# Shared expert: last inner chunk with gate and up in one stationary tile, row transposes and logits issued later

## The chip, the cores and the metric

The kernel runs on one core of a Trainium2 chip. The metric is the device time of one execution in microseconds (us), the median of several runs; lower is better. The core has five engines with queues of their own: TensorE (PE; its weight loads are shown as PEld), VectorE (DVE), ScalarE (ACT), GpSimd (POOL) and SyncE (SP), which here only issues DMAs. They run in order and meet through semaphores.

## The reference, cut to what matters

x has 4 x 1024 rows of 256; the context has 77 keys per batch.

```python
x = x + tanh(g_xattn[0]) * xattn(layernorm(x), ctx, ctx, mask, w_q, b_q, w_k, b_k, w_v, b_v, w_o, b_o)  # 16 heads of 16
x = x + tanh(g_ffn[0]) * ffn(layernorm(x), gate_w, eg, eu, ed, sg, su, sd)

def ffn(x, ...):                                   # H = 256, I = 688, 4 experts, top 2
    scores = softmax(xf @ gate_w.T)                # the logits
    topk_w, topk_idx = top_k(scores, 2)            # normalised, spread into comb[n, e]
    y = sum_e comb[:, e] * ((silu(xf @ eg[e].T) * (xf @ eu[e].T)) @ ed[e].T)
    y = y + (silu(xf @ sg.T) * (xf @ su.T)) @ sd.T # the shared expert
```

## The kernel before, in words

There are three parts, one after the other: `attend_and_share` (attention, the second layernorm, the router's logits and the shared expert), `route_and_prepare` (top-2 routing and the experts' weights) and `feed_forward` (the routed experts, 67 tiles). The change touches the first alone.

The rows are cut into NU = 16 units of 256 rows (two tiles of 128). A software pipeline of 20 steps runs over them, and each engine has a `step(i)` of its own whose order is written out by hand. In step i, TensorE does for unit i the scores (four groups, j = 0 to 3), for unit i-1 the transposes of the probabilities (`prob_T`, five groups through the one bank `p_t`) and the product with the values (`prob_v`), for unit i-2 the output projection, the transposes of the normalised rows (`xn_T`, L893) and the logits (`logits`, L904), for unit i-3 the shared expert's gate and up products (`gate_up`, L913, six chunks c of the inner dimension), for unit i-4 the down product (`down`, L933), and for unit i+1 the transposes and the product for q. Steps 3 to 15 have all but the ends of this. Several of these go through the one PSUM bank `p_m` in turn: x_T, q_T (read by q_hi on ScalarE, L463, and q_lo on VectorE, L656), xn_T (read by `xn_copies` on ScalarE, L496), logits (read by `lg_copy`, L504), prob_v and the output projection. `prob_v(n)` waits until `lg_copy` has read the bank.

Matrix products of f32r data are made of three passes (high x high, high x low, low x high parts). The inner dimension of 688 is five chunks of 128 and one of FT = 48 rows. `gate_up(n, c)` does 2 (gate, up) x 2 (halves of 256) x 3 passes = 12 matmuls into one bank of `p_f`, gate in columns 0 to 255 and up in 256 to 511. In the last chunk the stationary tile holds the 48 weight columns twice (at 0 and at LO_AT = 64), so that the hidden rows appear twice; rows 64 to 111 of the last chunk of `hT[0]` then carry the low part (`last_lo`, L701, on VectorE), and `down` needs two matmuls for it in place of three.

After a chunk ScalarE takes the tanh (`gate`, L509), VectorE multiplies twice (`inner`, L690), ScalarE makes the high part (`h_hi`, L514) and GpSimd the low part (`h_lo`, L357). `half_max(n, j)` (L669, VectorE) makes the row maxima of a score group, `exps` (L471, ScalarE) the exponentials, `t_copy(n, g)` (L486, ScalarE) moves a group of transposed probabilities out of `p_t`, after which `prob_T(n, g + 1)` may start. `normalise` (L337) and `xn_lo` (L350) are GpSimd's. `gate_up(n, c)` waits until `inner(n, c - 2)` is done, its bank being free then; `down` waits for `h_lo` and `last_lo`.

The order of step(i) on TensorE around the change is: scores 2, gate_up 2, xn_T, prob_T 3, gate_up 3, logits, prob_T 4, scores 3, gate_up 4, gate_up 5, prob_v; then scores 0 of the next step, down, output projection. On ScalarE: t_copy 2, normed_2, h_hi 1, q_hi, gate 2, xn_copies, four exponentials of group 2, t_copy 3, gate 3, h_hi 2, lg_copy, the other four, t_copy 4, gate 4, h_hi 3, four exponentials of group 3, gate 5, h_hi 4, the last four, h_hi 5, normed. On VectorE: q_lo, half_max 2, inner 2, stats_1, inner 3, recip 2, half_max 3, inner 4, inner 5, no_sight, recip 3, last_lo.

Of the kernel before, what the change touches and what calls it, by code (L numbers as in the profile page):

```python
# [47 lines left out]

XR = 6
NE = N * TOPK // P  # L50
EG = 8
# [61 lines left out]
def attend_and_share(nc, allocator, v):  # L113
# [6 lines left out]
    with st:  # L120
# [110 lines left out]
        def w_group(w):  # L231
# [4 lines left out]
            return "d", 0, 2 * (w - 8), 2  # L236

        W_AT = {0: 6, 1: 5}

# [71 lines left out]
        def _(pool):  # L311
# [73 lines left out]
            for s in range(2):  # L385
                pool.memset(wgu[s][:, :, :, FF:FF + P // 2 - FT].bitcast(fp32), 0.0).then_inc(s_wpad, 1)
                pool.memset(wgu[s][:, :, :, FC * P - P // 2 + FT:FC * P].bitcast(fp32), 0.0).then_inc(s_wpad, 1)
            pool.memset(tail[:, :, :], 0.0).then_inc(s_wpad, 1)
            residual_bias(0)

# [7 lines left out]
            def step(i):  # L398
                if i == 1:
                    down_tail()  # L400
                if has(i + 1):
                    residual_bias(i + 1)
                if has(i - 2):
                    rstd2(i - 2)
                if has(i):
                    normalise(i, 0)
                if has(i - 3):
                    h_lo(i - 3, 0)
                if has(i):
                    normalise(i, 1)  # L410
                if has(i - 3):
                    h_lo(i - 3, 1)
                if has(i - 2):
                    xn_lo(i - 2)
                if has(i - 3):
                    h_lo(i - 3, 2)
                if has(i):
                    normalise(i, 2)
                if has(i - 3):
                    h_lo(i - 3, 3)  # L420
                if has(i + 2):
                    rstd1(i + 2)
                if has(i - 3):
                    h_lo(i - 3, 4)
                if i % UB in (1, 2) and i // UB + 1 < B:

                    b = i // UB + 1
                    wait(pool, s_S, 4 * UB * (b - 1))
                    for m in range(KC):
                        key_block(b, i % UB - 1, m, s_kbnext)  # L430
                if has(i):
                    normalise(i, 3)
# [5 lines left out]
        def _(act):  # L438
# [70 lines left out]
            def gate(n, c):  # L509
                act.wait_ge(s_F, FC * n + c + 1)  # L510
                wait(act, s_hid, FC * n + c - 1)
                act.activation(th[:, c % 2, :], f_bank(f_use(n, c))[:, 0:UT * P], ACT.Tanh, scale=0.5).then_inc(s_th, 1)

            def h_hi(n, c):  # L514
                act.wait_ge(s_hid, FC * n + c + 1)
                wait(act, s_D, n)
                act.activation(hT[0][:, c, :], hid[:, c, :], ACT.Copy).then_inc(s_hhi, 1)  # L517

            def w_hi(w):
# [6 lines left out]
                else:  # L526
                    j = "gu".index(kind)
                    full = min(FF - c0 * P, cn * P)
                    last = act.activation(wgu[0][:, k, j, c0 * P:c0 * P + full], bank[:, 0:full], ACT.Copy)
                    if c0:  # L530
                        at = FC * P - P // 2
                        last = act.activation(wgu[0][:, k, j, at:at + FT], bank[:, at - c0 * P:at - c0 * P + FT],
                                              ACT.Copy)
                last.then_inc(s_whi, 1)
# [20 lines left out]
            def step(i):  # L555
# [31 lines left out]
                for w in weights_in(i)[2:4]:  # L587
                    w_hi(w)
                if has(i - 2):
                    xn_copies(i - 2)  # L590
                if has(i):
# [6 lines left out]
                if has(i - 2):  # L598
                    lg_copy(i - 2)
                if has(i):  # L600
# [3 lines left out]
                if has(i - 3):  # L604
                    gate(i - 3, 4)
                    h_hi(i - 3, 3)
                if has(i):
                    exps(i, 3, 0, HH // 2)
# [16 lines left out]
        def _(dve):  # L625
# [64 lines left out]
            def inner(n, c):  # L690
                bank = f_bank(f_use(n, c))
                dve.wait_ge(s_th, FC * n + c + 1)
                nc.vector.scalar_tensor_tensor(out=ah[:, c % 2, :], in0=th[:, c % 2, :], scalar=1.0,
                                               in1=bank[:, 0:UT * P], op0=ALU.add, op1=ALU.mult).then_inc(s_ah, 1)
                dve.wait_ge(s_ah, FC * n + c + 1)
                if c < FC - 1:
                    wait(dve, s_hlo, (FC - 1) * (n - 1) + c + 1)
                nc.vector.tensor_tensor(hid[:, c, :], bank[:, UT * P:2 * UT * P], ah[:, c % 2, :],  # L698
                                        ALU.mult).then_inc(s_hid, 1)

            def last_lo(n):  # L701
                dve.wait_ge(s_hhi, FC * (n + 1))
                nc.vector.tensor_tensor(hT[0][LO_AT:P, FC - 1, :], hid[LO_AT:P, FC - 1, :], hT[0][LO_AT:P, FC - 1, :],
                                        ALU.subtract).then_inc(s_hlast, 1)

# [7 lines left out]
            def w_lo(w):  # L713
# [6 lines left out]
                else:  # L720
                    j = "gu".index(kind)
                    full = min(FF - c0 * P, cn * P)
                    last = nc.vector.tensor_tensor(wgu[1][:, k, j, c0 * P:c0 * P + full], bank[:, 0:full],
                                                   wgu[0][:, k, j, c0 * P:c0 * P + full], ALU.subtract)
                    if c0:
                        at = FC * P - P // 2
                        last = nc.vector.tensor_tensor(wgu[1][:, k, j, at:at + FT],
                                                       bank[:, at - c0 * P:at - c0 * P + FT],
                                                       wgu[0][:, k, j, at:at + FT], ALU.subtract)
                last.then_inc(s_wlo, 1)  # L730
# [89 lines left out]
        def _(pe):  # L820
# [92 lines left out]
            def gate_up(n, c):  # L913
                if c == 0:
                    pe.wait_ge(s_xnlo, n + 1)
                    pe.wait_ge(s_wlo, 11)
                    pe.wait_ge(s_wpad, 5)
                    wait(pe, s_hid, FC * n)
# [5 lines left out]
                bank = f_bank(f_use(n, c))  # L924
                for j in range(2):
                    for k in range(KC):
# [21 lines left out]
            def w_T(w):  # L948
# [15 lines left out]
                else:  # L964
                    for c in range(c0, c0 + cn):
# [3 lines left out]
                        else:  # L969
                            for at in (0, P // 2):  # L970
                                last = nc.tensor.transpose(bank[:, (c - c0) * P + at:(c - c0) * P + at + FT],
                                                           raw[kind][0:FT, c * H + k * P:c * H + (k + 1) * P],
                                                           ident[0:FT, 0:FT])
                last.then_inc(s_wtr, 1)
# [30 lines left out]
            def step(i):  # L1005
# [28 lines left out]
                for w in weights_in(i)[2:4]:  # L1034
                    w_T(w)
                if has(i - 2):
                    xn_T(i - 2)
                if has(i - 1):
# [3 lines left out]
                if has(i - 2):  # L1042
                    logits(i - 2)
                if has(i - 1):
# [3 lines left out]
                if has(i - 3):  # L1048
                    gate_up(i - 3, 4)
                    gate_up(i - 3, 5)  # L1050
                for w in weights_in(i)[4:]:
# [610 lines left out]
```

## Time and profile before

| | us |
|---|---|
| median of 3 runs | 1085.26 (1084.17 to 1085.97) |
| profiled execution | 1084.47 |
| its span | 1082.6 |

| engine | busy us | share of the span | instructions |
|---|---|---|---|
| PE | 971.2 | 90% | 6399 |
| PEld | 870.2 | 80% | 6400 |
| DVE | 561.7 | 52% | 1255 |
| ACT | 498.8 | 46% | 1806 |
| POOL | 471.4 | 44% | 641 |

The page gives the shares of the whole span. `attend_and_share` takes about the first 540 us, `feed_forward` runs from about 619 us to the end, and in both TensorE is busy over nine tenths of the time. The share of busy time is a mean over stages, so it doesn't say which wait ends last in a step; the timeline of one step does. In rows of the timeline the number in square brackets is the time that the engine stood idle before the instruction, and what ended it. Durations overlap: the next matmul may start before the one before it has ended.

### The profile page before, as it was taken

To read this page: it belongs to the slowest core of one execution; us is meant where nothing else is said; L and a number is where in the kernel's file an instruction comes from. 1 tells how busy PE (TensorE), PEld (TensorE's weight loads), DVE (VectorE), ACT (ScalarE), POOL (GpSimd) and SP (SyncE) were. 2 spreads that over 40 slices of the span, in tenths; PEclk is the share of its full clock that TensorE was granted. 3 is DMA by queue.
4 is the path that set the end of the run, shared out by engine and by line. 5 is a ranking of instruction groups with operands and counts; after the bars stand their busy time and mean duration, and the time that the engine had idled before them with its cause. 6 is when DMAs were issued, how large, how long until landed. Compare 5 with 4: busy or idle time off the path is not lost. (4 is left out here: it accounts for less than half of the span.)

```text
span 1082.6 us, 21517 instructions
## 1 busy us (share of the span) xinstructions
PE 971.2 (90%) x6399; PEld 870.2 (80%) x6400; DVE 561.7 (52%) x1255; ACT 498.8 (46%) x1806; POOL 471.4 (44%) x641
## 2 busy tenths in 40 slices
PE   5678999999999999999747599999999999999995
PEld 3457888888888888888636489999999999999995
DVE  4555555556565565643389544444444444444442
ACT  3777676677776767663122222222222222222221
POOL 4345445545554444333107434444444444444442
PEclk9789999999999999999956699999999999999999
DMA  5100102100111110000053112222222222222221
GB/s 175 34 18 14 34 3 57 33 19 26 36 33 33 33 33 21 11 30 21 21 181 105 51 25 39 39 39 39 39 40 40 40 39 39 39 40 37 44 39 20
DMA packets 47646, 44.92 MB, mean 41 GB/s; under 512 B 14618, under 2 KB 44159, under 8 KB 47583
## 3 DMA queue, kind: packets, MB, share of 16 engines
q0 software_dynamic: 12864, 17.57, 10.0%
q1 hardware_dynamic: 33655, 26.37, 8.1%
q8 instruction: 31, 0.51, 0.2%
q10 hardware_dynamic: 1064, 0.21, 0.1%
q14 instruction: 32, 0.26, 0.1%
HBM read 26.39 MB, written 17.43 MB: 40 GB/s over the span
## 5 line engine op out<-in xcount | busy, mean ns | idle before, releaser
L1482 POOL DMA_INDIRECT out_rows<-yout,add_at x67 | 107.2, 1600 | 200.7 <-DVE yout L1540 200.7
L480 ACT ACTIVATE prob<-p_s,negmax 128x77 f32<-128x77 f32 x512 | 160.7, 349 | 40.1 <-DVE negmax L681 38.7
L1549 DVE TENSOR_TENSOR hid<-p_gu,sil 128x688 f32<-128x688 f32 x67 | 58.6, 875 | 168.9 <-ACT sil L1517 168.9
L1517 ACT ACTIVATE sil<-p_gu 128x688 f32<-128x688 f32 x67 | 50.0, 747 | 197.0 <-PE p_gu L1583 197.0
L480 ACT ACTIVATION_READ_ACCUMULATOR prob<-p_s,negmax 128x1 f32 x512 | 118.0, 231 | 0.0
L928 PE MATMUL p_f<-xnT_hi,swgu_hi 128*128 128x256 f32 x384 | 116.0, 302 | 1.0 <-DVE shid L698 0.9
L1583 PE MATMUL p_gu<-wgu_hi,fxT_hi 128*128 x402 | 112.6, 388 | 1.0 <-DVE fxT_lo L1534 1.0
L928 PE MATMUL p_f<-xnT_hi,swgu_lo 128*128 128x256 f32 x384 | 108.4, 282 | 0.0
L928 PE MATMUL p_f<-xnT_lo,swgu_hi 128*128 128x256 f32 x384 | 108.4, 282 | 0.0
L1583 PE MATMUL p_gu<-wgu_hi,fxT_lo 128*128 x402 | 106.7, 373 | 0.0
L1583 PE MATMUL p_gu<-wgu_lo,fxT_hi 128*128 x402 | 106.6, 374 | 0.0
L341 POOL TENSOR_TENSOR prob<-prob,rinv 128x616 f32<-128x616 f32 x64 | 77.9, 1217 | 58.5 <-DVE rinv L688 58.4
L1593 PE MATMUL p_y<-wd_hi,hT_hi 128*128 x335 | 100.3, 299 | 2.3 <-DVE hT_hi L1562 2.3
L1522 ACT ACTIVATE hT_hi<-p_h 128x512 fp32r<-128x512 f32 x67 | 40.1, 599 | 127.0 <-PE p_h L1607 127.0
L1593 PE MATMUL p_y<-wd_hi,hT_lo 128*128 x335 | 94.7, 283 | 0.0
L1593 PE MATMUL p_y<-wd_lo,hT_hi 128*128 x335 | 94.0, 281 | 0.0
L1471 POOL DMA_INDIRECT xin<-xn_scratch,get_at x67 | 67.7, 1010 | 55.5 <-POOL get_at L1468 51.6
L360 POOL TENSOR_TENSOR shT_lo<-shid,shT_hi 128x256 fp32r<-128x256 f32 x80 | 58.5, 731 | 63.0 <-ACT shT_hi L517 62.9
L1583 PEld LDWEIGHTS p_gu<-wgu_hi,fxT_lo 128*128 128x128 f32 x402 | 72.8, 190 | 12.6
L1583 PEld LDWEIGHTS p_gu<-wgu_lo,fxT_hi 128*128 128x128 f32 x402 | 72.5, 189 | 12.0
L928 PEld LDWEIGHTS p_f<-xnT_hi,swgu_hi 128*128 128x128 f32 x384 | 72.9, 190 | 9.0 <-issue 5.1
L1583 PEld LDWEIGHTS p_gu<-wgu_hi,fxT_hi 128*128 128x128 f32 x402 | 69.5, 191 | 10.3 <-issue 1.4
(234 smaller groups left out, 2467.5 us busy)
## 6 DMA issues: line engine op xcount, KB each, us to landing
xr<-in_x SPq DMA_DIRECT2D x16, 256.0 KB, 3.1
xn_scratch<-xn SPq DMA_DIRECT2D x16, 256.0 KB, 2.1
out_rows<-syout SPq DMA_DIRECT2D x16, 256.0 KB, 2.2
raw<-in_L_ffn_ed SPq DMA_DIRECT2D x4, 688.0 KB, 4.2
raw<-in_L_ffn_eg SPq DMA_DIRECT2D x4, 640.0 KB, 4.1
raw<-in_L_ffn_eu SPq DMA_DIRECT2D x4, 640.0 KB, 4.1
mask_in<-in_mask_Bx1xSxS_if SPq DMA_DIRECT2D x16, 77.0 KB, 2.6
xin<-xn_scratch,get_at POOLq DMA_INDIRECT x67, 2.7
```

Source lines behind the costliest of these rows:

```text
L341: pool.tensor_tensor(pr, pr, rinv[:, t, m * HH:(m + 1) * HH].unsqueeze(2).broadcast_to([P, HH, SK]), ALU.mult).then_inc(s_P, 1)
L360: pool.tensor_tensor(hT[1][:, c, :], hid[:, c, :], hT[0][:, c, :], ALU.subtract).then_inc(s_hlo, 1)
L480: last = act.activation(prob[n % 2][t][:, m * PW + h * SK:m * PW + (h + 1) * SK], p_s[:, 2 * t + h // 4, col:col + SK], ACT.Exp, bias=negm ...
L928: last = nc.tensor.matmul(bank[:, j * UT * P:(j + 1) * UT * P], wgu[w][:, k, j, c * P:(c + 1) * P], xns[x][:, n % 2, k, :], start=(k == 0 ...
L1471: pool.indirect_dma_start(xin[k][:, :], None, xn_d, bass.IndirectOffsetOnAxis(get_at[k][:, :], 0)).then_inc(s_gat[k], 16)
L1482: pool.indirect_dma_start(out, bass.IndirectOffsetOnAxis(add_at[k][:, :], 0), yout[k][:, :], None, compute_op=ALU.add).then_inc(s_add, 16)
L1517: act.activation(sil[:, :], p_gu[:, 0:FF], ACT.Silu).then_inc(s_sil, 1)
L1522: act.activation(hT[0][:, 0:4, :], p_h[:, 0, :].rearrange("p (c t) -> p c t", t=P), ACT.Copy)
L1549: nc.vector.tensor_tensor(hid[:, 0:FF], p_gu[:, FF:2 * FF], sil[:, :], ALU.mult).then_inc(s_hid, 1)
L1583: last = nc.tensor.matmul(p_gu[:, g0:g1], fxT[a][:, c, :], wgu[b][:, bass.ds(e * KC + c, 1), g0:g1], start=(c == 0 and q == 0), stop=(c == ...
L1593: nc.tensor.matmul(p_y[:, 0:H], hT[a][:, c, :], wd[b][:, bass.ds(e * FC + c, 1), :], start=(c == 0 and q == 0), stop=False)
```

## The change

In the last chunk of `gate_up` the stationary tile now holds the 48 gate columns at 0 and the 48 up columns at 64 (LAST_UP), and one group of 6 matmuls in place of 12 gives both: gate in partitions 0 to 47 and up in 64 to 111 of the same 256 columns. `gate`, `h_hi`, `inner` and `last_lo` work on 48 partitions in that chunk, and the padding of the tiles and of `hT[0]` is cleared accordingly. In the orders, TensorE issues xn_T after gate_up 3 (before: after gate_up 2) and the logits after gate_up 4 (before: after gate_up 3); ScalarE does xn_copies after h_hi 2 and lg_copy after h_hi 3; GpSimd does xn_lo after h_lo 3. The two functions that copy the shared weights out of PSUM (w_hi and w_lo) take their pieces from w_pieces; they are left out of the diff.

```diff
@@ -47,6 +47,7 @@
 PASSES = ((0, 0), (0, 1), (1, 0))
 
 XR = 6
+LAST_UP = (FC - 1) * P + LO_AT
 NE = N * TOPK // P
 EG = 8
 NSP = NS + 1
@@ -235,6 +236,17 @@
                 return kind, k, 4 * part, 4 - 2 * part
             return "d", 0, 2 * (w - 8), 2
 
+        def w_pieces(w, k, j, c0, cn, bank):
+
+            whole = min(cn, FC - 1 - c0) * P
+            if c0 + cn < FC:
+                yield w[:, k, j, c0 * P:c0 * P + whole], bank[:, 0:whole]
+            elif j == 0:
+                yield w[:, k, j, c0 * P:FF], bank[:, 0:FF - c0 * P]
+            else:
+                yield w[:, k, j, c0 * P:c0 * P + whole], bank[:, 0:whole]
+                yield w[:, k, 0, LAST_UP:LAST_UP + FT], bank[:, whole:whole + FT]
+
         W_AT = {0: 6, 1: 5}
 
         def weights_in(i):
@@ -383,9 +395,10 @@
                 key_block(0, 1, m, s_kblo)
             rstd1(1)
             for s in range(2):
-                pool.memset(wgu[s][:, :, :, FF:FF + P // 2 - FT].bitcast(fp32), 0.0).then_inc(s_wpad, 1)
-                pool.memset(wgu[s][:, :, :, FC * P - P // 2 + FT:FC * P].bitcast(fp32), 0.0).then_inc(s_wpad, 1)
+                pool.memset(wgu[s][:, :, 0, FF:LAST_UP].bitcast(fp32), 0.0).then_inc(s_wpad, 1)
+                pool.memset(wgu[s][:, :, 0, LAST_UP + FT:FC * P].bitcast(fp32), 0.0).then_inc(s_wpad, 1)
             pool.memset(tail[:, :, :], 0.0).then_inc(s_wpad, 1)
+            pool.memset(hT[0][:, FC - 1, :].bitcast(fp32), 0.0).then_inc(s_wpad, 1)
             residual_bias(0)
 
             def down_tail():
@@ -410,14 +423,14 @@
                     normalise(i, 1)
                 if has(i - 3):
                     h_lo(i - 3, 1)
+                if has(i - 3):
+                    h_lo(i - 3, 2)
+                if has(i):
+                    normalise(i, 2)
+                if has(i - 3):
+                    h_lo(i - 3, 3)
                 if has(i - 2):
                     xn_lo(i - 2)
-                if has(i - 3):
-                    h_lo(i - 3, 2)
-                if has(i):
-                    normalise(i, 2)
-                if has(i - 3):
-                    h_lo(i - 3, 3)
                 if has(i + 2):
                     rstd1(i + 2)
                 if has(i - 3):
@@ -509,12 +522,15 @@
             def gate(n, c):
                 act.wait_ge(s_F, FC * n + c + 1)
                 wait(act, s_hid, FC * n + c - 1)
-                act.activation(th[:, c % 2, :], f_bank(f_use(n, c))[:, 0:UT * P], ACT.Tanh, scale=0.5).then_inc(s_th, 1)
+                r = P if c < FC - 1 else FT
+                act.activation(th[0:r, c % 2, :], f_bank(f_use(n, c))[0:r, 0:UT * P], ACT.Tanh,
+                               scale=0.5).then_inc(s_th, 1)
 
             def h_hi(n, c):
                 act.wait_ge(s_hid, FC * n + c + 1)
                 wait(act, s_D, n)
-                act.activation(hT[0][:, c, :], hid[:, c, :], ACT.Copy).then_inc(s_hhi, 1)
+                r = P if c < FC - 1 else FT
+                act.activation(hT[0][0:r, c, :], hid[0:r, c, :], ACT.Copy).then_inc(s_hhi, 1)
 
             def w_hi(w):
                 kind, k, c0, cn = w_group(w)
...
@@ -586,8 +598,6 @@
                     gate(i - 3, 2)
                 for w in weights_in(i)[2:4]:
                     w_hi(w)
-                if has(i - 2):
-                    xn_copies(i - 2)
                 if has(i):
                     exps(i, 2, 0, HH // 2)
                 if has(i - 1):
@@ -596,7 +606,7 @@
                     gate(i - 3, 3)
                     h_hi(i - 3, 2)
                 if has(i - 2):
-                    lg_copy(i - 2)
+                    xn_copies(i - 2)
                 if has(i):
                     exps(i, 2, HH // 2, HH)
                 if has(i - 1):
@@ -604,6 +614,8 @@
                 if has(i - 3):
                     gate(i - 3, 4)
                     h_hi(i - 3, 3)
+                if has(i - 2):
+                    lg_copy(i - 2)
                 if has(i):
                     exps(i, 3, 0, HH // 2)
                 if has(i - 3):
@@ -689,19 +701,22 @@
 
             def inner(n, c):
                 bank = f_bank(f_use(n, c))
+                if c < FC - 1:
+                    r, up = P, bank[:, UT * P:2 * UT * P]
+                else:
+                    r, up = FT, bank[LO_AT:LO_AT + FT, 0:UT * P]
                 dve.wait_ge(s_th, FC * n + c + 1)
-                nc.vector.scalar_tensor_tensor(out=ah[:, c % 2, :], in0=th[:, c % 2, :], scalar=1.0,
-                                               in1=bank[:, 0:UT * P], op0=ALU.add, op1=ALU.mult).then_inc(s_ah, 1)
+                nc.vector.scalar_tensor_tensor(out=ah[0:r, c % 2, :], in0=th[0:r, c % 2, :], scalar=1.0,
+                                               in1=bank[0:r, 0:UT * P], op0=ALU.add, op1=ALU.mult).then_inc(s_ah, 1)
                 dve.wait_ge(s_ah, FC * n + c + 1)
                 if c < FC - 1:
                     wait(dve, s_hlo, (FC - 1) * (n - 1) + c + 1)
-                nc.vector.tensor_tensor(hid[:, c, :], bank[:, UT * P:2 * UT * P], ah[:, c % 2, :],
-                                        ALU.mult).then_inc(s_hid, 1)
+                nc.vector.tensor_tensor(hid[0:r, c, :], up, ah[0:r, c % 2, :], ALU.mult).then_inc(s_hid, 1)
 
             def last_lo(n):
                 dve.wait_ge(s_hhi, FC * (n + 1))
-                nc.vector.tensor_tensor(hT[0][LO_AT:P, FC - 1, :], hid[LO_AT:P, FC - 1, :], hT[0][LO_AT:P, FC - 1, :],
-                                        ALU.subtract).then_inc(s_hlast, 1)
+                nc.vector.tensor_tensor(hT[0][LO_AT:LO_AT + FT, FC - 1, :], hid[0:FT, FC - 1, :],
+                                        hT[0][0:FT, FC - 1, :], ALU.subtract).then_inc(s_hlast, 1)
 
             def result(n):
                 dve.wait_ge(s_D, n + 1)
...
@@ -922,7 +932,7 @@
                 else:
                     pe.wait_ge(s_hid, FC * n + c - 1)
                 bank = f_bank(f_use(n, c))
-                for j in range(2):
+                for j in range(2 if c < FC - 1 else 1):
                     for k in range(KC):
                         for q, (w, x) in enumerate(PASSES):
                             last = nc.tensor.matmul(bank[:, j * UT * P:(j + 1) * UT * P],
@@ -967,10 +977,9 @@
                             last = nc.tensor.transpose(bank[:, (c - c0) * P:(c - c0 + 1) * P],
                                                        raw[kind][:, c * H + k * P:c * H + (k + 1) * P], ident[:, :])
                         else:
-                            for at in (0, P // 2):
-                                last = nc.tensor.transpose(bank[:, (c - c0) * P + at:(c - c0) * P + at + FT],
-                                                           raw[kind][0:FT, c * H + k * P:c * H + (k + 1) * P],
-                                                           ident[0:FT, 0:FT])
+                            last = nc.tensor.transpose(bank[:, (c - c0) * P:(c - c0) * P + FT],
+                                                       raw[kind][0:FT, c * H + k * P:c * H + (k + 1) * P],
+                                                       ident[0:FT, 0:FT])
                 last.then_inc(s_wtr, 1)
 
             pe.wait_ge(s_id, 2)
@@ -1033,20 +1042,21 @@
                     gate_up(i - 3, 2)
                 for w in weights_in(i)[2:4]:
                     w_T(w)
+                if has(i - 1):
+                    prob_T(i - 1, 3)
+                if has(i - 3):
+                    gate_up(i - 3, 3)
                 if has(i - 2):
                     xn_T(i - 2)
                 if has(i - 1):
-                    prob_T(i - 1, 3)
-                if has(i - 3):
-                    gate_up(i - 3, 3)
+                    prob_T(i - 1, 4)
+                if has(i):
+                    scores(i, 3)
+                if has(i - 3):
+                    gate_up(i - 3, 4)
                 if has(i - 2):
                     logits(i - 2)
-                if has(i - 1):
-                    prob_T(i - 1, 4)
-                if has(i):
-                    scores(i, 3)
-                if has(i - 3):
-                    gate_up(i - 3, 4)
+                if has(i - 3):
                     gate_up(i - 3, 5)
                 for w in weights_in(i)[4:]:
                     w_T(w)
```

## Rows read from the trace of the kernel before

**Rows 1.** Busy us by engine in a stretch; then granted clock, DMA share, GB/s.
```profile
100.00:450.00 350.00, 327.91 (x2367) 294.21 (x2367) 207.45 (x441) 250.63 (x1088) 167.04 (x226) 1.00 0.10 29
```
**Rows 2.** Waits of PE in 150 to 450 us: total, times, longest.
```profile
PE p_m L900 <- DVE qT_lo L659: 14.4, 10, 1.6
PE p_t L866 <- ACT pT L489: 3.2, 10, 0.3
```
**Rows 3.** Timeline of PE: start, us, instruction, idle before it.
```profile
231.86 0.38 PE L879 MATMUL p_m<-pT,vblk 128*128 128x256 f32 x1
...
252.09 0.28 PE L928 MATMUL p_f<-xnT_hi,swgu_lo 128*128 128x256 f32 x1
253.78 0.63 PE L900 MATMUL p_m<-ident,xn 128*128 128x128 f32 x4 [1.41 <-DVE qT_lo L659]
...
256.11 0.95 PE L909 MATMUL p_m<-gwT,xnT 128*128 128x4 f32 x8
257.39 0.63 PE L866 MATMUL p_t<-ident,prob 128*128 128x128 f32 x4 [0.32 <-ACT pT L489]
...
260.11 0.28 PE L928 MATMUL p_f<-xnT_hi,swgu_hi 128*128 128x256 f32 x1
...
261.55 0.81 PE L879 MATMUL p_m<-pT,vblk 128*128 128x256 f32 x3
...
266.58 0.38 PE L941 MATMUL p_f<-swd_hi,shT_hi 128*128 128x256 f32 x1
```
**Rows 4.** Timeline of ACT in the same step.
```profile
252.53 0.47 ACT L512 ACTIVATE th<-p_f 128x256 f32<-128x256 f32 x1
254.44 0.60 ACT L500 ACTIVATE xnT<-p_m 128x512 f32<-128x512 f32 x1 [1.45 <-PE p_m L900]
254.94 0.59 ACT L502 ACTIVATE xnT_hi<-p_m 128x512 fp32r<-128x512 f32 x1
255.41 0.33 ACT L480 ACTIVATE prob<-p_s,negmax 128x77 f32<-128x77 f32 x1
...
256.61 0.63 ACT L489 ACTIVATE pT<-p_t 128x512 f32<-128x512 f32 x1
...
257.72 0.39 ACT L480 ACTIVATE prob<-p_s,negmax 128x77 f32<-128x77 f32 x1
```
**Rows 5.** Timeline of DVE: last_lo of step 6, then the same step, then step 16.
```profile
205.21 0.70 DVE L703 TENSOR_TENSOR shT_hi<-shid,shT_hi 64x256 fp32r<-64x256 f32 x1
...
252.76 0.88 DVE L659 SCALAR_TENSOR_TENSOR qT_lo<-p_m,bq,qT_hi 128x256 fp32r<-128x256 f32 x2 [2.30 <-ACT qT_hi L467]
...
254.44 0.80 DVE L681 TENSOR_REDUCE negmax<-p_s 128x8 f32<-128x616 f32 x1
...
259.15 0.20 DVE L688 RECIPROCAL rinv<-rowsum 128x8 f32<-128x8 f32 x1 [0.72 <-ACT prob L480]
...
264.58 1.48 DVE L703 TENSOR_TENSOR shT_hi<-shid,shT_hi 64x256 fp32r<-64x256 f32 x1
...
493.31 0.42 DVE L703 TENSOR_TENSOR shT_hi<-shid,shT_hi 64x256 fp32r<-64x256 f32 x1 [0.48 <-ACT shT_hi L517]
```
**Rows 6.** Timeline of POOL at the end of the same step.
```profile
264.56 1.22 POOL L341 TENSOR_TENSOR prob<-prob,rinv 128x616 f32<-128x616 f32 x1 [0.66 <-DVE rinv L688]
```
**Rows 7.** Timeline of PE in steps 9 and 16.
```profile
290.46 0.39 PE L928 MATMUL p_f<-xnT_hi,swgu_hi 128*128 128x256 f32 x1 [0.50 <-DVE shid L698]
...
484.81 0.33 PE L900 MATMUL p_m<-ident,xn 128*128 128x128 f32 x1 [0.38 <-ACT xn L454]
```
**Rows 8.** Busy us by engine around two falls of the granted clock (columns as rows 1).
```profile
70.00:74.00 4.00, 1.85 (x15) 1.23 (x14) 3.24 (x8) 3.58 (x18) 2.10 (x5) 0.98 0.01 4
74.00:77.00 3.00, 2.97 (x9) 2.60 (x10) 0.20 (x1) 3.00 (x18) 0.45 (x2) 0.50 0.00 0
528.00:531.00 3.00, 0.62 (x6) 0.62 (x6) 1.26 (x3) 1.10 (x3) 0.84 (x2) 1.00 0.00 0
531.00:534.00 3.00, 3.00 (x17) 3.00 (x17) 0.00 (x0) 0.00 (x0) 0.00 (x0) 0.54 0.02 5
```

More of the change, by code:

```diff
@@ L412, in step @@
                     h_lo(i - 3, 1)
-                if has(i - 2):
-                    xn_lo(i - 2)
                 if has(i - 3):
@@ L420, in step @@
                     h_lo(i - 3, 3)
+                if has(i - 2):
+                    xn_lo(i - 2)
                 if has(i + 2):
@@ L527, in w_hi @@
                     j = "gu".index(kind)
[L528 to L533, printed above, removed]
+                    for dst, src in w_pieces(wgu[0], k, j, c0, cn, bank):
+                        last = act.activation(dst, src, ACT.Copy)
                 last.then_inc(s_whi, 1)
@@ L588, in step @@
                     w_hi(w)
-                if has(i - 2):
-                    xn_copies(i - 2)
                 if has(i):
@@ L606, in step @@
                     h_hi(i - 3, 3)
+                if has(i - 2):
+                    lg_copy(i - 2)
                 if has(i):
@@ L721, in w_lo @@
                     j = "gu".index(kind)
[L722 to L729, printed above, removed]
+                    for (dst, src), (hi, _) in zip(w_pieces(wgu[1], k, j, c0, cn, bank),
+                                                   w_pieces(wgu[0], k, j, c0, cn, bank)):
+                        last = nc.vector.tensor_tensor(dst, src, hi, ALU.subtract)
                 last.then_inc(s_wlo, 1)
@@ L916, in gate_up @@
                     pe.wait_ge(s_wlo, 11)
-                    pe.wait_ge(s_wpad, 5)
+                    pe.wait_ge(s_wpad, 6)
                     wait(pe, s_hid, FC * n)
@@ L1035, in step @@
                     w_T(w)
-                if has(i - 2):
-                    xn_T(i - 2)
                 if has(i - 1):
@@ L1042, in step @@
                 if has(i - 2):
-                    logits(i - 2)
+                    xn_T(i - 2)
                 if has(i - 1):
@@ L1049, in step @@
                     gate_up(i - 3, 4)
+                if has(i - 2):
+                    logits(i - 2)
+                if has(i - 3):
                     gate_up(i - 3, 5)
```

## The prediction

> **What bounds the kernel now.** I read first the busy time by stretches. In 100 to 450 us, where the full steps 3 to 14 of the attention and shared-expert stage run, TensorE is busy 327.91 of 350 us at full clock and no other engine passes 251 [rows 1]. So TensorE sets the pace, but not alone: the table of waits has three causes of its idle time there, and two of them come once in each step: 1.4 us before the row transposes (L900, waiting for the low half of q) and 0.3 us before a transpose of probabilities (L866, waiting for ScalarE's copy out of `p_t`) [rows 2]. The reader who sees the first will want to hide it. The question is which of the two waits ends last, and the timeline of one step (i = 8; its prob_v starts 261.55 - 231.86 = 29.69 us after the one before) answers it. From gate_up(2)'s last matmul at 252.09 to the logits at 256.11 lie 4.02 us, 1.57 of them empty before L900 (252.09 plus a slot of 0.12, to 253.78). After the logits TensorE stands again until 257.39, when the fourth copy of `p_t` is there [rows 3]. So the copy ends last, with 0.32 us to spare over the first wait.
>
> What sets that copy: ScalarE works in order. It does the tanh of chunk 2 (252.53), the two copies of the transposed rows (until about 255.4), four exponentials (255.41) and then the `p_t` copy (256.61) [rows 4]. The exponentials need the row maximum, a VectorE reduction from 254.44 to 255.24, and that stands behind q_lo (252.76), which waited 2.30 us for ScalarE's q_hi [rows 5]. Everything on this path (q_hi, q_lo, maximum, exponentials, `p_t` copy) hangs on ScalarE's unbroken work since prob_T(1), and the change touches none of it.
>
> **The change part by part.** I take times of that step and shift them.
>
> Moved: xn_T behind gate_up(3). The stretch up to prob_T(4) keeps prob_T(3), gate_up(3) and xn_T: of the 4.02 less 0.12 us, 1.57 were stall, so 2.33 of work, which now ends at 252.21 + 2.33 = 254.54 in the queue, some 254.7 with the last matmul's tail. q_lo is ready at 253.64, so the old wait is gone [rows 3, 5]. What is late next is prob_T(4). On ScalarE the copies of the rows are no longer ahead of the exponentials, which start when the maximum is ready, 255.28 in place of 255.41; the `p_t` copy follows 1.20 later, and prob_T(4) starts at 257.26 in place of 257.39 [rows 3, 4]. TensorE therefore stands for one stretch of 257.26 - 254.7, about 2.5 us, where it had 1.41 and 0.32. The gain of the move is 0.13 us a step.
>
> Moved: logits behind gate_up(4). They ran in time that would have been empty before prob_T(4); now they stand behind it. Eight matmuls at 0.1 us, 0.8 us, plus 0.1 for the change of shape: +0.9 [rows 3]. They find their operand ready (the copies, 257.53 to 258.6).
>
> Removed: six of twelve matmuls of chunk 5. The last chunk takes 261.55 - 260.11 = 1.44 us for its twelve [rows 3]; half is -0.72. Sum from prob_T(4) on: -0.13 + 0.9 - 0.72 = +0.05 us for prob_v's start. In fact a tie.
>
> ScalarE after the `p_t` copy: the two row copies (2 x 0.5 us, as at 254.44 to 255.41) now stand before the second four exponentials: 257.72 becomes 258.50, +0.78 [rows 4]. Behind them wait the reciprocal (259.15 becomes 259.93), the last maximum, the last eight exponentials, gate 5, the last h_hi and VectorE's `last_lo` (264.58 becomes 265.36) [rows 5]. `last_lo` takes 1.48 us, because GpSimd's normalise started 0.02 us before it [rows 6]; alone it takes 0.42 (the row at 493.31) [rows 5]. So it ends at 266.84 instead of 266.06. `down` started at 266.58 and waits for it; its new natural start is 266.63, so it is held until about 266.91: +0.28 in ordinary steps. In steps 6 and 10 GpSimd does key blocks there and `last_lo` takes 0.70 (205.21) [rows 5]: no hold. lg_copy stands behind h_hi(3); it ends near 261.2 and prob_v may start at 261.6: hidden, with 0.4 to spare. GpSimd's xn_lo is moved behind h_lo(3), to about 262; its user is gate_up(0) of the next step, over 10 us on; h_lo(2), h_lo(3) and normalise(2) come no later for it. SP issues the same DMAs, keyed to normed_2, which is not moved.
>
> In steps 5 and 9 a load of x comes late, and chunk 5 waits 0.50 us for it through VectorE (290.46) [rows 7]. There the 0.78 is covered and the logits fill that 0.5: -0.55 each.
>
> Steps 15 to 18 have no new scores. In 16, 17 and 18 the chunk saves 0.72 each, and the wait of 0.38 at 484.81 goes too [rows 7]: -2.5 in all; step 15 I count at nothing. Steps 0 to 2: four fewer small transposes and two fewer pieces on ScalarE and VectorE, one more memset on GpSimd, all below 0.5 us together; counted at nothing, -0.5 to +0.5.
>
> Sum at full clock: 8 ordinary steps (3, 4, 7, 8, 11 to 14) x 0.33 + 2 x 0.05 - 2 x 0.55 - 2.5 = -0.9 us.
>
> **The clock.** A stall of 2.5 us in each step is new, and its price is not in that sum. The trace of before shows both sides. Stalls of 1.41 to 1.57 us in each of steps 3 to 14 never lowered the granted clock: 1.00 throughout [rows 1]. One stall of about 2.4 us, after the last chunk of step 18 (TensorE busy 0.62 of 3 us), was followed by 0.54 (the 1.2 GHz level), and two stalls that add to 2.15 us in 70 to 74 were followed by 0.50 for three us and more [rows 8]. Our 2.5 lies above both. A fall costs half of a stretch of about 3.4 us in which TensorE is the bound (prob_T(4), scores, two chunks, prob_v): 1.7 us, bounded by 1.2 (it begins inside the stall) and 1.8. In a step with a fall the +0.28 is swallowed, since TensorE is then later than `last_lo`, so a fall adds 1.4 in ordinary steps, 1.7 in the others: 1.5 on average. How many of the twelve steps have one is unknown. Zero is the lower bound, from the 1.57 that did nothing, twelve the upper. I take 7, because 2.5 is nearer to the rows that fell (2.4, 2.15) than to 1.57, but not far above them, so that some steps may be spared. 7 x 1.5 = +10.6.
>
> Forecast: -0.9 + 10.6 = +9.7 on the profiled execution of 1084.47 (span 1082.6), 1094.2. The median of the runs lies 0.8 above that execution, so 1095.0.
>
> **The rivals.**
>
> Full clock kept. If 2.5 us does not lower the clock, the sum is -0.9: 1084.4, no change. For it: 95 percent of each step is dense work. Against: rows 8. Chance 0.15. In between, one to three falls, 1085.9 to 1088.9: 0.08, half of it within 0.2%.
>
> Full clock and `last_lo` first. normalise and `last_lo` start 0.02 us apart. If the shift lets `last_lo` begin first it takes 0.42 us, `down` is not held, and 8 x 0.28 goes: -3.1, 1082.2, faster. It decides from the point at which h_lo(4) holds GpSimd past 265.36; I put h_lo(4)'s end at 265.35, so it is a coin's toss, but it needs the full clock as well: 0.07.
> The Trainium skill (SBUF — State Buffer, section SBUF: two separate sides) says the port pair shared by VectorE and GpSimd is an exclusive lock: the one that starts first has it for its whole instruction. By that rule this order of starts decides the 1.48 against the 0.42, and rows 5 and 6 agree with it; the sum at full clock would be -3.1 by it if the order turns, and -0.9 if it holds.
>
> The wait really goes. If the exponentials are not pinned by the maximum, or the copy of `p_t` comes as early as TensorE does, both waits (1.41 and 0.32) and the 0.72 come off, 2.5 us in twelve steps and 2.5 at the end: 1053. Against it: the reduction's end at 255.24, 0.17 before the first exponential, and nothing of its path is edited. Chance 0.04.
>
> **How the numbers follow.** Forecast (four or more falls) 0.66, own range 1090 (four) to 1102 (twelve). Faster by over 0.2%: 0.07 + 0.04 + 0.01 = 0.12. Within 0.2% (about what a measurement of this kernel can tell from no change): 0.15 + 0.04 = 0.19. Slower: 0.69. The range of 8 in 10 takes in the full-clock case and leaves out both faster ones and the last counts of falls: 1083.5 to 1101.
>
> **What would show it.** Between xn_T and prob_T(4) an idle stretch of 2.5 us put down to ScalarE's `p_t` copy, in every step from 3 to 14; the wait for q_lo gone; 6 x 16 = 96 fewer L928 matmuls; the first exponential of half 2 some 0.04 us behind the maximum; second exponentials 0.8 later against it; a granted clock below 1.00 in 100 to 450, with falls just behind that stall and prob_v stretched. Steps at full clock of 30.0 us, steps with a fall of 31.4. Wrong would be: a `p_t` copy that comes before 256.5 in the step's time, or a clock of 1.00 throughout; the first breaks the whole argument, the second only its last term.

## The result and the profile after

| | before | after |
|---|---|---|
| median of the runs, us | 1085.11 | 1132.68 (1131.94 to 1134.52) |
| span of the profiled execution, us | 1082.6 | 1130.1 |
| granted clock, mean over the span | 0.955 | 0.904 |

The ratio is 1.0443 (95% interval 1.0426 to 1.0459): 47.6 us slower. The forecast was slower, 1095.0 with a range up to 1101. The sign held and the size did not. The ratios of the experiments below are each to the kernel before as run beside them (medians 1085.25 to 1086.11 us).

First the stretch of rows 1, then TensorE's waits in 150 to 450 us, which answer to rows 2.

```profile
100.00:450.00 350.00, 321.60 (x2039) 287.17 (x2038) 186.86 (x400) 225.92 (x969) 153.07 (x204) 0.87 0.09 27
```
```profile
PE p_t L876 <- ACT pT L502: 23.1, 9, 2.6
```

In the same 350 us 2039 matmuls ran where there were 2367 (some 60 of the difference are the chunk's own saving, six a step), at a granted clock of 0.87 in place of 1.00. All three waits of before have become one: TensorE waits for the `p_t` copy, 2.6 us in each step. The timelines of one step, TensorE, then ScalarE, then VectorE, answer to rows 3 to 5; take 18.58 us off each time to lay it over the step shown there.

```profile
272.66 0.60 PE L910 MATMUL p_m<-ident,xn 128*128 128x128 f32 x4
...
275.82 1.09 PE L876 MATMUL p_t<-ident,prob 128*128 128x128 f32 x4 [2.56 <-ACT pT L502]
...
280.64 1.70 PE L919 MATMUL p_m<-gwT,xnT 128*128 128x4 f32 x8
...
283.62 5.44 PE L889 MATMUL p_m<-pT,vblk 128*128 128x256 f32 x20
```
```profile
273.86 0.33 ACT L493 ACTIVATE prob<-p_s,negmax 128x77 f32<-128x77 f32 x1 [2.27 <-DVE negmax L693]
...
275.07 0.61 ACT L502 ACTIVATE pT<-p_t 128x512 f32<-128x512 f32 x1
...
276.12 0.62 ACT L513 ACTIVATE xnT<-p_m 128x512 f32<-128x512 f32 x1
```
```profile
273.02 0.80 DVE L693 TENSOR_REDUCE negmax<-p_s 128x8 f32<-128x616 f32 x1
```

Moved to the old step's time (259.64 - 241.06 = 18.58 between their output projections), the exponentials start at 255.28, the `p_t` copy at 256.49 and prob_T(4) at 257.24. The forecast had 255.28, 256.48 and 257.26. Up to here the forecast is right to 0.02 us. What follows is not: the eight logits matmuls take 1.70 us, not 0.95 [rows 3], and prob_v 5.44, not 4.48. The kernel before, in its step:

```profile
261.55 4.48 PE L879 MATMUL p_m<-pT,vblk 128*128 128x256 f32 x20
```

The stretches around the stall in the changed kernel show why (columns as in rows 1).

```profile
275.00:276.00 1.00, 0.18 (x1) 0.21 (x2) 0.53 (x4) 1.00 (x5) 0.00 (x0) 0.66 0.00 0
276.00:279.00 3.00, 3.00 (x15) 2.36 (x15) 1.32 (x4) 2.95 (x12) 0.95 (x2) 0.50 0.00 0
279.00:282.00 3.00, 3.00 (x17) 3.00 (x16) 2.05 (x4) 0.69 (x2) 1.35 (x2) 0.50 0.00 0
282.00:285.00 3.00, 3.00 (x12) 2.73 (x13) 0.77 (x3) 2.43 (x14) 2.84 (x7) 0.50 0.01 3
285.00:288.00 3.00, 3.00 (x14) 2.63 (x13) 2.07 (x4) 2.14 (x9) 2.81 (x3) 0.91 0.00 0
```

A mean of 0.66 over 275 to 276 puts the fall at 275.3, still inside the stall; 0.91 over 285 to 288 puts the return at 285.5. The clock is at the lower level (1.2 GHz) for 10.2 us. Two earlier steps of the same execution had a short fall:

```profile
142.00:146.00 4.00, 3.91 (x20) 3.30 (x21) 2.03 (x5) 3.21 (x13) 1.69 (x2) 0.57 0.00 0
146.00:150.00 4.00, 4.00 (x28) 3.76 (x27) 2.50 (x6) 3.42 (x19) 2.93 (x6) 1.00 0.00 0
```

The second of them: the low lasts 3.4 us (0.57 over 4 us) and begins just after the stall's end (142.09). Taken from one output projection to the next, those steps are 31.58 and 31.19 us long, and the ten steps behind them 34.13 to 34.23. The 47.5 us of the spans divide so: the start, up to step 3's output projection, 2.8; the two steps with a short fall 3.0; the ten with a long one 43.1; steps 15 and 16 -1.6; the rest of the kernel, steps 17 and 18 in it, 0.2.

### The profile page after: what moved, and what is told of

It is laid out like the page before. It is cut to its first block and busy times, and to the rows that moved or that the text cites. A ratio compares the mean times of both kernels' runs of the same rounds, so it can differ in the third digit from the quotient of the medians.

```text
span 1130.1 us, 21314 instructions
## 1 busy us (share of the span) xinstructions
PE 1008.9 (89%) x6299; PEld 901.9 (80%) x6300; DVE 563.5 (50%) x1253; ACT 500.0 (44%) x1804; POOL 475.1 (42%) x642
## 5 line engine op out<-in xcount | busy, mean ns | idle before, releaser
L493 ACT ACTIVATION_READ_ACCUMULATOR prob<-p_s,negmax 128x1 f32 x512 | 113.4, 221 | 0.0
L876 PE MATMUL p_t<-ident,prob 128*128 128x128 f32 x320 | 55.5, 302 | 43.1 <-ACT pT L502 43.1
L889 PE MATMUL p_m<-pT,vblk 128*128 128x256 f32 x320 | 84.4, 426 | 0.5 <-ACT lg L519 0.5
L938 PEld LDWEIGHTS p_f<-xnT_hi,swgu_hi 128*128 128x128 f32 x352 | 75.7, 215 | 9.5 <-issue 8.4
```

The source lines that it names most:

```text
L493: last = act.activation(prob[n % 2][t][:, m * PW + h * SK:m * PW + (h + 1) * SK], p_s[:, 2 * t + h // 4, col:col + SK], ACT.Exp, bias=negm ...
L876: last = nc.tensor.transpose(p_t[:, (k * UT + t) * P:(k * UT + t + 1) * P], prob[n % 2][t][:, c * P:(c + 1) * P], ident[:, :])
L889: last = nc.tensor.matmul(p_m[:, m * UT * P:(m + 1) * UT * P], vblk[:, b % 2, c, :], pT[:, c, :], start=(c % CH == 0), stop=(c % CH == CH ...
L938: last = nc.tensor.matmul(bank[:, j * UT * P:(j + 1) * UT * P], wgu[w][:, k, j, c * P:(c + 1) * P], xns[x][:, n % 2, k, :], start=(k == 0 ...
```

## The experiments

Steps are counted by their output projections on TensorE. "A low" is a stretch at the 1.2 GHz level. Its beginning and length are read from the granted clock in finely cut stretches. Steps with no fall and no late load of x are called ordinary, if GpSimd makes no key blocks in them.

**One part alone: the chunk.** The changed kernel with TensorE's, ScalarE's and GpSimd's old orders.

```diff
-prob_T 3; gate_up 3; xn_T; prob_T 4; scores 3; gate_up 4; logits; gate_up 5
+xn_T; prob_T 3; gate_up 3; logits; prob_T 4; scores 3; gate_up 4; gate_up 5
```

> Only the new last chunk (6 matmuls in place of 12); all orders as before. Theory S (the 2.56 us stall of the moved order brings the clock down; the tile itself is harmless): no stall over 1.6 us, clock 1.00 in steps 3 to 14, each step 0.72 us shorter than 29.69, in all 16 x 0.72 = 11.5 us off: about 1074. Rival T (the new tile, with 48 of 128 partitions in use twice, is what lowers the clock): clock below 1.00 in each step, 1100 or more.

Measured: 1077.35 us, ratio 0.9928 (0.9909 to 0.9948). Its stretch of rows 1 and its wait for `last_lo` in it:

```profile
100.00:450.00 350.00, 326.49 (x2349) 291.52 (x2348) 212.18 (x452) 251.88 (x1098) 168.84 (x231) 1.00 0.10 30
```
```profile
PE p_f L951 <- DVE shT_hi L718: 1.9, 8, 0.3
```

The clock stays at 1.00. The tile is harmless, and it is the part that gains. Ordinary steps take 29.24 us, not 28.97: TensorE arrives earlier and now waits 0.27 us for `last_lo` before `down` (the second row). That is the hold that the forecast had placed in the changed kernel; with it the total came out 3 us above my 1074.

**The other part alone: the orders.** The kernel before with the new orders and its 12 matmuls in the last chunk.

> Only the new orders; the last chunk with its 12 matmuls. Theory S: the stall of 2.5 us before prob_T 4 and a fall of the clock in each step, as in the changed kernel; 1130 to 1145, the period 34.1 us (if the clock's fall and the step are locked to each other) or 34.9 (if they are not, 0.72 us more work). Rival T: clock 1.00 and about 1095.

Measured: 1111.3 us, ratio 1.0232 (1.0211 to 1.0253). So the orders cost, as the theory had it. But this kernel does 0.72 us more work in each step than the changed one and is 21 us faster; neither of my two numbers was that. Every step has the stall of 2.57 us (2.75 to 2.77 in steps 3 and 14); step 3 has a short fall, step 4 none, and from step 5 on only each third has one, of 10.2 us. Two steps in turn, the stall ending at 238.26 and at 268.70:

```profile
231.00:236.00 5.00, 4.69 (x39) 4.21 (x38) 2.39 (x5) 3.02 (x9) 1.95 (x2) 1.00 0.16 52
236.00:240.00 4.00, 1.74 (x14) 1.42 (x15) 2.76 (x9) 3.71 (x16) 0.74 (x1) 1.00 0.01 2
268.00:269.00 1.00, 0.30 (x2) 0.33 (x3) 0.53 (x4) 1.00 (x5) 0.00 (x0) 0.56 0.00 0
269.00:278.00 9.00, 9.00 (x43) 8.36 (x42) 3.41 (x7) 4.94 (x23) 5.09 (x8) 0.50 0.01 3
278.00:282.00 4.00, 4.00 (x19) 3.47 (x19) 2.82 (x5) 3.19 (x13) 2.48 (x3) 0.96 0.00 0
```

Steps without a fall take 30.43 us, steps with one 34.76: a long low costs 4.3 us.

**The stall filled.** Behind xn_T, 20 more matmuls of 128x256 into the bank that scores 3 overwrites; then the same with 8.

```diff
 xn_T(i - 2)
+for _ in range(20):   # 8 in the second
+    matmul(p_s[:, 2, 0:256], wgu[0][:, 0, 0, 0:128], xns[0][:, (i - 3) % 2, 0, :], start=True, stop=True)
```

> The changed kernel with 20 more matmuls of 128x256 (2.4 us at full clock) behind xn_T in steps 3 to 15; what they write is overwritten by scores 3. Theory S: the stall is filled, the clock stays at 1.00, the step takes 30.0 us (the time of my sum at full clock), total 1084 to 1087, though there is more work. Rival P (the step is longer because its path is longer: logits, row copies and last_lo behind prob_T 4; the clock only follows): no gain, 1130 or more.

Measured: 1088.48 us, ratio 1.003 (1.0016 to 1.0045), 1.5 above my range; the clock at 1.00 in steps 3 to 14, ordinary steps 30.03 us. Twenty matmuls more in each step, and 44 us less than the changed kernel. The path is as long as it was; only the idle time is gone. So the clock is the cause, and the forecast's 29.69 + 0.33 = 30.02 for a step at full clock is measured as 30.03, with the wait for `last_lo` at its 0.3 (waits in 100 to 450 us):

```profile
100.00:450.00 350.00, 344.01 (x2512) 311.20 (x2510) 205.68 (x442) 248.35 (x1082) 165.55 (x227) 1.00 0.10 29
```
```profile
PE p_t L876 <- ACT pT L502: 2.6, 12, 0.4
PE p_f L951 <- DVE shT_hi L718: 2.6, 9, 0.3
```

> As the run before with 8 matmuls: the stall is cut from 2.56 to about 1.6 us, the length that did nothing in the kernel before. Theory S with a limit between 1.6 and 2.5 us: clock 1.00, 1084 to 1088. If any stall at this place lowers the clock (because light work surrounds it: transposes, scores, logits): clock below 1.00 in some or all steps, 1095 to 1133.

Measured: 1092.31 us, ratio 1.0071 (1.0046 to 1.0095). That lies between my two numbers. The profiled execution is the slowest of the three (1096.44). In it nine of the twelve steps keep the clock. The stall is 1.79 us in step 3, which has a low of 3.4 us, 1.82 us in step 14, which has one of 6.8 us, and 1.6 us in the ten others, of which one, step 10, has a low of 6.8 us. The two steps with the longer low are 3 us longer. So the limit is not sharp at this place: 1.6 us is mostly, not always, spared.

**Is it locked?** The changed kernel with two more matmuls (0.24 us) ahead of scores 3, the stall left as it is.

> The changed kernel with two more matmuls of 128x256 (0.24 us) ahead of scores 3 in steps 3 to 15; the stall stays at 2.56 us. Theory L (lock: a step with a 10.2 us low comes out at 34.14 us and so meets the next change of the clock at the same place, so that every step falls; another length of step breaks this): with 0.24 us more per step some steps have no fall, 1 in 3 or more, and the kernel is faster for more work: 1105 to 1125. Rival F (each stall of this length brings a fall, whatever the step's length): a fall in each step, 3 us more work: about 1136.

Measured: 1102.06 us, ratio 1.0171 (1.0107 to 1.0234). More work in each step, and about 31 us less than the changed kernel. It did not come about quite as theory L had it: the total lies 3 us below my range, and only three of the twelve steps have no fall, not one in three or more. Of the nine others six have a low of 3.4 us, two of 6.8 and one of 10.2, so most of the gain is from shorter lows. The spread of its runs is wide (1099.4 to 1112.9). Two neighbouring steps, stalls ending at 205.98 and 237.41, both of 2.57 us:

```profile
205.00:210.00 5.00, 4.02 (x21) 3.52 (x22) 2.81 (x9) 4.11 (x17) 1.79 (x2) 0.66 0.00 2
237.00:242.00 5.00, 4.59 (x39) 4.30 (x40) 2.95 (x8) 4.41 (x17) 2.37 (x3) 1.00 0.01 2
```

So a stall of this length doesn't bring the clock down each time. In the changed kernel the ten long lows begin 34.13 to 34.14 us apart, and the steps between them settle at 34.13 to 34.14 us: a step with a long low ends with the next stall in the same place against the low, so the next step has a long low too. A step that is a little longer or shorter walks out of that place. It went into it the same way: the two short lows of the changed kernel began 0.57 and 0.11 us behind the stall's end, the next 0.37 us ahead of it, and from there on all ten were long. That the place of the stall against the clock's changes decides is argued from these times and from two kernels whose steps have another length; no run moves the place alone.

**What makes a low long?** Two experiments. In the first, the logits stand behind gate_up 5 and lg_copy behind gate 5.

> The changed kernel with the logits behind gate_up 5 and lg_copy behind gate 5; the stall stays. Theory G (light work, the eight logits matmuls of 4 columns foremost, inside the low stretch keeps the clock down: 10.2 us in place of 3.4): lows that begin before the stall's end last 3.4 or 6.8 us. Rival W (the place of the low's beginning against the stall alone decides): those lows still last 10.2 us. The total depends on how often the clock falls: 1090 to 1135.

Measured: 1135.52 us (two runs), ratio 1.046 (1.0425 to 1.0494). It tells less than I wanted. The lows at the stall last 3.4 us, but all of them begin behind its end (0.1 to 0.6 us in eight steps, 1.4 and 1.5 us in two), where they were short before too. Step 5 has no low, and step 11 only one, of 6.8 us, at another place. A second low of 3.4 us follows in six of the twelve steps, after a new idle time of 1.0 us, in which prob_v waits for lg_copy, and that wait of itself makes the steps longer. One of the steps with two lows:

```profile
278.00:282.00 4.00, 3.66 (x19) 3.18 (x20) 1.99 (x6) 3.46 (x14) 1.44 (x2) 0.60 0.00 0
282.00:285.00 3.00, 2.18 (x19) 2.09 (x17) 1.83 (x5) 2.29 (x13) 2.03 (x3) 0.97 0.01 3
285.00:290.00 5.00, 4.81 (x15) 3.94 (x16) 1.51 (x5) 2.85 (x12) 4.84 (x8) 0.66 0.01 3
```

In the second, the logits' eight matmuls of 4 columns are replaced by seven of 256 columns at the same place. This kernel leaves out the router's logits.

> The changed kernel with the logits' eight matmuls of 4 columns replaced by seven of 128x256 into unused columns of the bank (the logits are left out, so the routing works on other values); at full clock it is 0.84 us against about 0.8. Theory G (light work inside the low stretch keeps the clock down): lows that begin before the stall's end last 3.4 or 6.8 us in place of 10.2, the lock at 34.14 us is not reached, 1095 to 1120. Rival W (the place of the low's beginning against the stall decides its length): lows of 10.2 us in nearly every step, steps of 34.1, about 1132.

Measured: 1104.13 us, ratio 1.0159 (1.0131 to 1.0187). All twelve steps have a fall. Ten lows last 3.4 us and begin at the stall's end or up to 1.3 us behind it. The lows that began ahead of the stall's end (by 0.33 and 0.42 us) lasted 6.8 us, not 10.2. One of them, from 205.1 to 211.9:

```profile
205.00:208.00 3.00, 2.61 (x12) 2.00 (x13) 1.07 (x4) 3.00 (x14) 0.73 (x1) 0.51 0.01 3
208.00:212.00 4.00, 4.00 (x21) 4.00 (x20) 2.71 (x5) 1.27 (x5) 2.01 (x3) 0.51 0.00 0
212.00:216.00 4.00, 4.00 (x23) 3.59 (x22) 1.73 (x5) 4.00 (x22) 3.84 (x7) 1.00 0.00 0
```

TensorE is busy for the whole of the low behind the stall in both kernels; what differs is the shape of these matmuls. With the logits in place, 17 lows in three kernels (the changed one, the one with the orders alone, the one with two more matmuls) began 0.37 to 0.83 us ahead of the stall's end, and 15 of them lasted 10.2 us. The two others, 6.8 us, are in the kernel that has two more dense matmuls inside the low. So light work inside a low seems to lengthen it from 6.8 to 10.2 us, and the logits, put behind gate_up 4, are part of that. It rests on two lows here and two there, and no run shows it alone. What makes 6.8 us of 3.4 is open. In these four kernels the lows that began ahead of the stall's end were the longer ones, with what is left of the stall, the transposes and the scores inside them; but in the kernel with 8 more matmuls both lows of 6.8 us began behind it (1.8 and 1.5 us). What exactly sets the length stays open.

**The hold on `last_lo`.** The chunk alone, with `last_lo` ahead of `recip(i, 3)` on VectorE, so that GpSimd's normalise starts after it.

```diff
-recip(i, 3); last_lo(i - 3)
+last_lo(i - 3); recip(i, 3)
```

> The first experiment (new chunk, old orders) with last_lo ahead of recip 3 on VectorE, so that GpSimd's normalise 3 starts behind it. Theory P (last_lo held by normalise is what took 0.27 us a step there): last_lo takes 0.42 us, TensorE's wait for it is gone, ordinary steps 28.97 us in place of 29.24, total 1074 to 1075. Rival: the hold is by ScalarE's last h_hi, not by normalise: no change, 1077.

Measured: 1075.05 us, ratio 0.9906 (0.9889 to 0.9922), ordinary steps 28.96 us, the wait gone. `last_lo` before this swap and after it, in the same step:

```profile
231.79 1.47 DVE L718 TENSOR_TENSOR shT_hi<-shid,shT_hi 48x256 fp32r<-48x256 f32 x1
```
```profile
231.55 0.42 DVE L718 TENSOR_TENSOR shT_hi<-shid,shT_hi 48x256 fp32r<-48x256 f32 x1 [0.62 <-ACT shT_hi L533]
```

In the first, GpSimd's normalise (1.22 us) had started 0.02 us before it; in the second it started 0.31 us behind its end. The Trainium skill's page SBUF — State Buffer (section SBUF: two separate sides) says of the port pair that VectorE and GpSimd share that the one that starts first has it for its whole instruction. The trace agrees where GpSimd is first: `last_lo` then ends 0.27 us behind normalise.

**The cause of the stall.** The changed kernel with the `p_t` copy ahead of the exponentials that wait for the maximum (and `last_lo` first, as above). ScalarE's order from gate 2 on (exps 2a and 2b are the first and the second four exponentials of group 2):

```diff
-exps 2a; t_copy 3; gate 3; h_hi 2; xn_copies; exps 2b; t_copy 4; gate 4; h_hi 3
+t_copy 3; xn_copies; exps 2a; gate 3; h_hi 2; t_copy 4; exps 2b; gate 4; h_hi 3
```

> The changed kernel with ScalarE's order mended: the copy of p_t (t_copy 3) ahead of the exponentials of group 2, xn_copies behind it, t_copy 4 ahead of the second four; last_lo ahead of recip 3. Theory S (the stall hangs on the p_t copy standing behind exponentials that wait for the row maximum): prob_T 4 waits for nothing, no stall above 1 us, clock 1.00, steps of 28.0 to 28.6 us, total 1060 to 1068. Rival (the stall is of another kind, so the order of the copy does not matter): 1120 or more.

Measured: 1076.27 us, ratio 0.9917 (0.9901 to 0.9934). prob_T 4 waits for nothing, and ordinary steps take 28.43 us: the stall was the copy's place in ScalarE's queue. The total missed, 8 us above my range. Steps 5 and 9 took 31 us, with a wait of 2 us before gate_up 5 and a low each; the steps behind them, 6 and 10, took 29.5 us, with a wait of 1.0 us for `last_lo`; and in the ordinary ones prob_v waits 0.8 us for lg_copy.

> The experiment with the early p_t copy, and two more changes of order: stats_1 (which waits for a late load of x in steps 5 and 9) behind half_max 3 on VectorE, lg_copy ahead of the second four exponentials on ScalarE. If the waits for shid (up to 2.2 us in steps 5 and 9) and for lg_copy (0.8 us a step) are what kept that version at 28.43 us and 31, they go, as do the two falls of the clock: steps of 27.6 to 28.4 us, total 1064 to 1071. If another wait stands right behind them: 1074 to 1077.

Measured: 1096.79 us, ratio 1.0089 (1.0061 to 1.0117), outside both of my ranges. My mend opened another stall: `last_lo` came 2.0 to 2.8 us late for `down` in steps 3 to 13 (1.7 in step 14), and each of steps 4 to 13 has a low with it, of 3.4 us in eight and of 6.8 in two.

```profile
274.49 0.54 PE L952 MATMUL p_f<-swd_hi,shT_hi 128*128 128x256 f32 x1 [2.02 <-DVE shT_hi L719]
```
```profile
274.00:278.00 4.00, 3.51 (x17) 3.54 (x18) 2.08 (x4) 3.18 (x16) 2.45 (x2) 0.57 0.04 4
278.00:282.00 4.00, 4.00 (x30) 3.74 (x29) 0.75 (x1) 0.74 (x6) 0.00 (x0) 1.00 0.06 5
```

It repeats the finding elsewhere in the step: a stall of 2.0 us lowers the clock there too, though one of 2.4 us, in step 3, did not. Here dense work follows, and most of the lows are short. Last, the kernel with the early copy, with the small DMAs that place the values spread over three steps and issued behind the load of x:

> The kernel with the early p_t copy (1076.3), with the small DMAs that place the values of the next batch spread over three steps and issued behind the load of x, so that the load is not late in steps 5 and 9. If the late load is what makes the waits of 2 us and the two falls of the clock there: steps 5 and 9 at about 28.4 to 28.8 us, the steps after them at 28.4, clock 1.00 in steps 3 to 14, total 1067 to 1070. If the DMAs delay something else, or the wait of 2 us has another cause: 1074 to 1080.

Measured: 1071.75 us, ratio 0.9869 (0.9845 to 0.9894), the clock at 1.00 in steps 3 to 14. The 2 us waits and the falls are gone, but the total is 2 to 5 us above what I expected: in each of steps 5, 6, 9 and 10, in which GpSimd makes key blocks, `down` waits 1.0 us for `last_lo` (in the version before only in 6 and 10), and they take 29.5 us. `last_lo` and the key block start within 0.01 us of each other there, and `last_lo` takes 1.5 us: the same hold. It is the fastest of those run: 13.5 us less than before, 61 less than the changed kernel.

## Why the prediction was wrong, point by point

- What bounds the step: right. The `p_t` copy ended last, hiding the first wait gained 0.15 us (forecast 0.13), and the new stall was 2.56 us against 2.5.
- The sum of a step at full clock, 29.69 + 0.33: right, shown by the filled stall (30.03 us), the hold on `last_lo` (0.3) included. Steps 5, 6 and 10 came out worse in that kernel: 6 and 10 have the hold too (+0.3 and +0.4 us, forecast +0.05), and step 5 waits 0.80 us for the late load (+0.3, forecast -0.55). Steps 3 to 14 came to +3.0 us together, where the sum had +1.6.
- That the stall lowers the clock: right; and that the clock's rival, a longer path alone, was not it.
- The price of a fall is the step that failed. 1.7 us from a low of 3.4 us, 1.4 in an ordinary step, was about right for short lows (31.19 - 30.02 = 1.2). It was wrong for the others. The term took its length from two lows of before with dense work behind them [rows 8]. Here the logits, transposes and scores follow, and the low lasted 10.2 us: 34.14 - 30.03 = 4.1 us. Half of 10.2 is 5.1; of that 0.3 are the wait for `last_lo`, which is swallowed, some 0.25 lie in the stall, and the light work did not take twice as long at the lower clock (the logits 1.70 us, where twice 0.95 is 1.90). Why the low lasts 10.2 us and not 3.4 stays open; the light work inside it has a part, as far as four lows show.
- How many steps fall: 7 assumed, all twelve measured, ten of them long. The twelve steps were treated as independent draws. They are not: ten in a row are of 34.13 to 34.23 us, and the length of a step decides where the next stall comes. Twelve falls were my upper end, at 1.5 us each, so the range ended at 1101 where 1084.4 + 2 x 1.2 + 10 x 4.1 would have given 1128.
- The rows that the count went by were not all. The kernel before has another stall of 2.4 us, in step 17, and the clock stayed at 1.00 through it and behind it, so a stall's length alone did not decide there either:

```profile
514.67 0.36 PE L941 MATMUL p_f<-swd_hi,shT_hi 128*128 128x256 f32 x1 [2.38 <-DVE shT_hi L703]
```
```profile
512.00:515.00 3.00, 0.62 (x6) 0.45 (x5) 1.46 (x4) 1.10 (x3) 1.12 (x2) 1.00 0.00 0
515.00:520.00 5.00, 5.00 (x44) 5.00 (x43) 0.75 (x1) 0.00 (x0) 0.00 (x0) 1.00 0.00 0
```

- The start, counted at nothing: 2.8 us. Step 2 has the same stall (2.83 us) and a low of 6.8 us where before it was 3.4. The filled kernel, which leaves that step alone, still has it, and it is 2.4 of the 3.8 us by which that kernel's span lies above my -0.9; 1.4 more are those of steps 3 to 14 above.
- The last steps: -2.5 expected in 16 to 18. Step 16 gained 1.3 us, and step 15, counted at nothing, 0.3. Steps 17 and 18 gained nothing (+0.25 up to the last stall before `down`, forecast -1.4): the stall of 2.4 us in step 17 now has a low of 3.4 us behind it (granted clock 0.57 over 562 to 566 us).
- The rival in which the whole wait goes needed the `p_t` copy out from behind the maximum. The early copy does that, and a step came to 28.43 us: 1.3 us less than before, not 2.5, with 0.8 us of it left as the wait for lg_copy.

The Trainium skill's page TensorE: Matmul & The Clock Gate (section HAM oscillation — how this bites in real kernels) describes a kernel in which a wait in every tile brings the clock down in every tile. Twelve lows in twelve steps here agree, though the waits there are of 3 to 5 us and here 2.56 us were enough. That kernels with a little more work in the step escape it in part (1111.3 and 1102.1) is what the runs add.

## What to carry to other kernels

Before moving an instruction behind a wait, find what the engine waits for next: two short stalls merged into one of 2.5 us cost 44 us here through the clock, though the path was 0.3 us a step longer. If TensorE must idle, try to let dense matmuls follow and to keep small ones (few columns, transposes) away from there; the runs speak for it and do not prove it. For the upper end of a forecast let a recurring stall bring its longest low in every step: steps that repeat are no independent draws. A kernel whose steps repeat exactly can stay locked to the clock's changes, and then a little more work in a step can make it faster.

## What was not expected of the hardware

- A low of the clock lasted 3.4, 6.8 or 10.2 us. Begun shortly ahead of the stall's end it was 10.2 us in 15 of 17 cases with the logits of 4 columns, and 6.8 in two of two with matmuls of 256 columns in their place, with TensorE busy throughout in both.
- Steps of 34.14 us and lows 34.14 us apart, ten in a row, the first steps up to 34.2: 0.24 us more work per step broke this, and 1132.7 us became 1102.1.
- A stall of 1.6 us left the clock alone in nine steps of ten; both of 1.8 us were followed by a low. One of 2.4 us did so in the kernel before (step 17), and one of 2.57 us in seven steps of ten where only the orders were changed.
